# Gate inputs of a GRU stored in memory by group of columns, in two parts, and loaded back as pieces of 6144 bytes

## The chip, the cores and the metric

The kernel runs on one core of one Trainium2 chip. The metric is device microseconds of one execution; several executions are timed and the median is given. Engines are named as the profile names them: PE is the matrix engine (PEld its weight loads), DVE the vector engine, ACT the scalar engine, POOL the general one, SP the sync engine, which here only issues transfers (SPq).

## What is computed

Two layers with a residual each, on x of 8 sequences x 512 tokens x 256 channels. The first is a mixture of experts (a shared gated MLP plus two chosen of eight experts), the second a GRU over the 512 tokens:

```
x = x + moe(x, cond)                       # tokens are independent
Xz, Xr, Xh = x @ Wxz.T + bxz, x @ Wxr.T + bxr, x @ Wxh.T + bxh
for each of the 512 tokens, in order:
    Z = sigmoid(xz + H @ Whz.T + bhz)
    R = sigmoid(xr + H @ Whr.T + bhr)
    H_tilda = tanh(xh + R * H @ Whh.T + bhh)
    H = Z * H + (1 - Z) * H_tilda
    Y = H @ Whq.T + bhq
x = x + Y
```

Xz, Xr and Xh with their biases are called the gate inputs below. They are the only thing that the change touches.

## The kernel before, in words

Tokens go in 32 tiles of 128 rows: 8 sequences x 16 tokens (B = 8, TS = 16). Each of the 512 steps of the GRU is a chain PE, ACT, DVE, PE, ACT, DVE; between its parts PE does matmuls of the first layer for a later pair of tiles, by a table written by hand (`place_of` gives the row r of the table for tile n and step s). Every engine has its own program, in order, and waits on semaphores.

The gate inputs of tile t are made one tile ahead of the scan. PE projects them into two banks (`project`, L962), DVE adds the bias of each half of the columns and writes it to `xproj` (`add_bias`, L761; q is 0 or 1, PIECES = 2, each time `xp_ready` goes up by one). `xproj` has 128 partitions, one for each token, and 4 groups of 192 columns (NG = 4, RW = 192; half q is groups 2q and 2q+1). The scan needs them the other way: `xs` holds sequence b of group j on partition 32 j + b, with the 16 tokens side by side. So SP stores `xproj` to a tensor in memory and loads it back in that form, in two halves of eight tokens (`gate_rows`, L409, four transfers for a half, one for each group). `xproj`, `xs` and others lie in the tensor that the profile calls gru_raw.

ACT copies a step's row of `xs` to the banks: `seed_r` (L535) for the reset gate, `seed_zc` (L543) for the others; PE adds the products with H to it. Before the first row of a tile is copied ACT waits for `xs_first`, before row 8 for `xs_second`. The first row of tile n+1 is copied in the last step of tile n. In ACT's program the copy stands between tanh of the update gate (L595) and the step's a_row (L604), on which DVE waits.

For an odd n the halves q = 0 and q = 1 of tile n+1 come in steps 9 and 11 of tile n (`BIAS2` rows 3 and 5), for an even n in steps 0 and 1 (rows 10 and 11). Half 0 of `xs` may be overwritten once step 7 is done, half 1 once the tile is.

Of the kernel before, what the change touches and what calls it, by code (L numbers as in the profile page):

```python
# [17 lines left out]
def moe_then_gru(nc, x, cond, router_w, router_b, w1, w3, w2, we1, we2,  # L18
                 wxz, bxz, whz, bhz, wxr, bxr, whr, bhr, wxh, bxh, whh, bhh, whq, bhq, out):
    F32 = mybir.dt.float32  # L20
# [5 lines left out]
    B, T, C = x.shape  # L26
    P = 128
# [9 lines left out]
    NG = 4  # L37
# [3 lines left out]
    GATES = 3  # L41
    RW = GATES * GW
# [4 lines left out]
    HALF = TS // 2  # L47

    ctx = ExitStack()
    with ctx:  # L50
# [3 lines left out]
        def sem(name):  # L54
            return ctx.enter_context(nc.semaphore(name))
# [60 lines left out]
        xproj = spent[:, 0:NG * RW].rearrange("p (j c) -> p j c", j=NG)  # L116
# [23 lines left out]
        r_ps, z_ps, c_ps = r_bank[:, 0:GW], zc_bank[:, 0:GW], zc_bank[:, GW:2 * GW]  # L140
        tr_ps = [r_bank, zc_bank]

        by_token = nc.dram_tensor("gate_inputs_by_token", [P, NG, RW], F32, kind="Internal").ap()


        ld_x = [sem(f"ld_x{i}") for i in range(2)]
# [23 lines left out]
        bias_ready = sem("bias_ready")  # L170
# [9 lines left out]
        x1T_ready = [sem(f"x1T_ready{i}") for i in range(2)]  # L180
        xp_done = sem("xp_done")
        xp_ready = sem("xp_ready")
        xp_stored = sem("xp_stored")
        xs_first = sem("xs_first")
        xs_second = sem("xs_second")

# [54 lines left out]
        def evacuate(m):  # L241

            kind, i = GROUPS[m]
            src = tr_ps[m % 2]
            if kind == "x":
                return xT_all[:, 2 * i:2 * i + 2, :, :].rearrange("p n k t -> p (n k t)"), src[:, 0:512], 1.0
            if kind == "cond":
                return condT[:, :, :].rearrange("p k t -> p (k t)"), src[:, 0:C], 1.0
            _, part, gate = WEIGHTS[i]
            s = WSCALE[part][gate]  # L250
            if part == "x":
                return wxT[:, :, :, COLS[gate]], src[:, 0:KC * C].rearrange("p (k j n) -> p k j n", k=KC, j=NG), s
            if part == "h":
                return whT[:, gate, :, :].rearrange("p k c -> p (k c)"), src[:, 0:KC * C], s
            return wqT[:, :, :].rearrange("p k c -> p (k c)"), src[:, 0:KC * C], s
# [12 lines left out]
        PIECES = 2  # L268
# [83 lines left out]
        def iterations(body):  # L352

            for n in range(NT + 1):
                body(n, *stages(n))
# [4 lines left out]
        @block.sync  # L360
        def _(sp):
            def load_x(i, tiles):

                for n in range(tiles.start, tiles.stop):
                    sp.dma_start(x_all[:, n, :], x[:, n * TS:(n + 1) * TS, :]).then_inc(ld_x[i], 16)

            def load_gru(r):

                sp.dma_start(raw[r][:, :, :], gru_w[r].rearrange("(o p) c -> p o c", p=P)).then_inc(ld_gru, 16)

            load_x(0, slice(0, 2))
            sp.dma_start(w1_raw, w1.rearrange("(k p) h -> p k h", p=P)).then_inc(ld_w13, 16)
            sp.dma_start(w3_raw, w3.rearrange("(k p) h -> p k h", p=P)).then_inc(ld_w13, 16)
            load_x(1, slice(2, EARLY))
            sp.dma_start(rw_sb[:, :, :], router_w.rearrange("(k p) e -> p k e", p=P)).then_inc(ld_router, 16)
            sp.dma_start(cond_tok[:, :], cond.rearrange("b (a c) -> b a c", a=1).to_broadcast([B, TS, C])).then_inc(ld_router, 16)
            sp.dma_start(rbias[:, :], router_b.rearrange("(a e) -> a e", a=1).to_broadcast([P, NE])).then_inc(ld_router, 16)
            sp.dma_start(we1_raw, we1.rearrange("e (k p) h -> p e k h", p=P)).then_inc(ld_we1, 16)
            sp.wait_ge(consts_ready, 1)
            for j in range(NG):  # L380
                sp.dma_start(h0_rows[Q * j:Q * j + B, :, :], cond[:, GW * j:GW * (j + 1)].rearrange("b (i q) -> b i q", i=NI)).then_inc(ld_h0, 16)
            for r, _, _ in WEIGHTS:
                load_gru(r)
            sp.dma_start(w2_sb[:, :, :], w2.rearrange("(k p) c -> p k c", p=P)).then_inc(ld_w2, 16)
            sp.dma_start(we2_sb[:, :, :, :], we2.rearrange("e (k p) c -> p e k c", p=P)).then_inc(ld_we2, 16)
            for gate in range(GATES):
                for dst, src in ((bias_rows, gate_bx[gate]), (bias_h, gate_bh[gate])):
                    sp.dma_start(dst[:, :, COLS[gate]], src.rearrange("(a j n) -> a j n", a=1, j=NG)
                                 .to_broadcast([P, NG, GW])).then_inc(ld_bias, 16)
            sp.dma_start(bias_q[:, :], bhq.rearrange("(a c) -> a c", a=1).to_broadcast([P, C])).then_inc(ld_bias, 16)  # L390

            def load_late(t):

                for j in range(NG):
                    for b in range(2):
                        for k in range(KC):
                            src = x[b::2, t * TS:(t + 1) * TS, k * P + Q * j:k * P + Q * (j + 1)].rearrange("i t c -> t i c")
                            sp.dma_start(x_blocks[Q * j + TS * b:Q * j + TS * (b + 1), t % 2, k, :]
                                         .rearrange("t (i c) -> t i c", i=NG), src).then_inc(ld_late[t % 2], 16)
                sp.dma_start(x_all[:, t, :], x[:, t * TS:(t + 1) * TS, :]).then_inc(ld_late[t % 2], 16)  # L400

            load_late(EARLY)
            load_late(EARLY + 1)

            def gate_rows(half, done):

                for j in range(NG):
                    src = by_token[:, j, :].rearrange("(b t) c -> b t c", b=B)[:, half * HALF:(half + 1) * HALF, :]
                    sp.dma_start(xs[Q * j:Q * j + B, half * HALF:(half + 1) * HALF, :], src).then_inc(done, 16)  # L409

            sp.wait_ge(xp_ready, PIECES)
            sp.dma_start(by_token, xproj[:, :, :]).then_inc(xp_stored, 16)
            sp.wait_ge(xp_stored, 16)
            sp.wait_ge(xs_zeroed, 1)
            gate_rows(0, xs_first)
            gate_rows(1, xs_second)
            sp.wait_ge(shared_ready, NSH)
            sp.wait_ge(we1_split, NE)

            def store_out(t):  # L420

                sp.wait_ge(y_ready, t + 1)
                sp.dma_start(out[:, t * TS:(t + 1) * TS, :], y_out[:, :]).then_inc(out_stored, 16)

            def body(n, scan, proj, outs):
                if n % 2 == 0 and n > 0:
                    store_out(n - 2)
                if proj:
                    t = n + 1
                    sp.wait_ge(xp_ready, PIECES * (t + 1))  # L430
                    sp.wait_ge(xs_second, 16 * NG * t)
                    sp.dma_start(by_token, xproj[:, :, :]).then_inc(xp_stored, 16)
                    sp.wait_ge(xp_stored, 16 * (t + 1))
                if proj:
                    sp.wait_ge(seeded_zc, TS * n + HALF)
                    gate_rows(0, xs_first)
                if n % 2 == 0 and n > 0:
                    store_out(n - 1)
                if proj:
                    sp.wait_ge(seeded_zc, TS * (n + 1))  # L440
                    gate_rows(1, xs_second)
                if n % 2 == 0 and n + EARLY + 2 < NT:
                    sp.wait_ge(late_xT_ready, n + 2)
                    load_late(n + EARLY + 2)
                    load_late(n + EARLY + 3)

            iterations(body)
            sp.wait_ge(out_stored, 16 * NT)

# [177 lines left out]
        def _(dve):  # L627
# [124 lines left out]
            def add_bias(t, q):  # L752

                dve.wait_ge(xp_done, PIECES * t + q + 1)
                if q == 0:
                    if t == 0:
                        dve.wait_ge(bias_ready, GATES)
                    else:
                        dve.wait_ge(xp_stored, 16 * t)
                cols = slice(q * PCOLS, (q + 1) * PCOLS)  # L760
                dve.tensor_tensor(xproj[:, :, :].rearrange("p j c -> p (j c)")[:, cols], dn_ps[q][:, 0:PCOLS],  # L761
                                  bias_rows[:, :, :].rearrange("p j c -> p (j c)")[:, cols], ALU.add).then_inc(xp_ready, 1)
# [68 lines left out]
            for q in range(PIECES):  # L831
                add_bias(0, q)
# [20 lines left out]
            def body(n, scan, proj, outs):  # L853
                for s in range(TS):
# [39 lines left out]
                    if r in BIAS2 and 0 <= 2 * p + BIAS2[r][1] < NT:  # L894
                        add_bias(2 * p + BIAS2[r][1], BIAS2[r][0])
# [315 lines left out]
```

## Time and profile before

| | |
|---|---|
| median of 3 executions | 1314.22 us (1314.08 to 1318.01) |
| the profiled execution | 1317.0 us, of it 1315.2 us span |
| busy | PE 97%, DVE 76%, ACT 61%, PEld 67%, POOL 1% |
| granted clock of PE, mean | 0.997 |
| moved by transfers | 51.39 MB, 39 GB/s on average |
| store of the gate inputs | 32 transfers of 384 KB, 2.4 us to landing (median) |
| loads of the gate inputs | 256 transfers of 48 KB |

The span is the time from the first to the last instruction on the core; the rest of the execution's time lies around it. Busy shares are means over a start of 75 us in which the first tiles and the weights are made ready, and a scan of 512 steps. In a wait, the name behind the arrow is what ended it.

### The profile page before, as it was taken

The numbers are of one execution on the slowest core, as the hardware profiler recorded it, in microseconds if no ns is written. First come the engines' busy times: TensorE is split into PE (matmuls) and PEld (weight loads), VectorE is DVE, ScalarE is ACT, GpSimd is POOL, SyncE is SP. The second block draws the span as 40 slices with busy tenths as digits, with TensorE's granted clock in tenths as the row PEclk, the third lists the DMA queues.
The fourth block names the chain that finished last, engine by engine and source line by source line (L and its number), as shares of the span: only waits on it lengthen the run. The fifth ranks groups of instructions, "written<-read, shape, count | busy, mean of one in ns | idle before, by whom it ended". The sixth has DMA issues, their size and how long they took to land.

```text
span 1315.2 us, 85216 instructions
## 1 busy us (share of the span) xinstructions
PE 1275.3 (97%) x36022; PEld 876.9 (67%) x36022; DVE 1005.0 (76%) x6121; ACT 799.5 (61%) x4384; POOL 7.6 (1%) x26
## 2 busy tenths in 40 slices
PE   8999999999999999999999999999999999999886
PEld 7667676767767676776767667666766767676443
DVE  3567878788787878778787877878787787877765
ACT  4156666666666666666666666666666666666554
POOL 1000000000000000000000000000000000000000
PEclk8999999999999999999999999999999999999999
DMA  8111112012111101211111121111111111010110
GB/s 266 33 45 22 48 23 43 25 30 51 25 50 23 42 25 30 50 25 49 23 39 30 30 51 24 50 21 37 33 30 44 25 43 30 18 38 14 44 20 11
DMA packets 79252, 51.39 MB, mean 39 GB/s; under 512 B 43032, under 2 KB 74264, under 8 KB 78872
## 3 DMA queue, kind: packets, MB, share of 16 engines
q1 hardware_dynamic: 78872, 45.95, 14.7%
q8 instruction: 284, 4.65, 1.6%
q14 instruction: 96, 0.79, 0.2%
HBM read 29.13 MB, written 16.78 MB: 35 GB/s over the span
## 4 chain that ended last, share of the span: by engine, by line
PE 88%; DVE 5%; ACT 3%; DMA 2%; issue 1%; SPq 0%
PE dn_ps L962 27%; PE up_ps L989 24%; PE zc_bank L1099 20%; PE r_bank L1099 14%; PE aux L962 2%; DVE terms L882 2%; DMA gru_raw<-gate_inputs_by_token 1%; ACT t_r L593 1%; DVE hist L885 1%; ACT t_h L613 1%; DVE t_rT L862 1%; PE misc L962 1%; DMA gate_inputs_by_token<-gru_raw 1%; DMA xT_all<-in_L_cond_w 1%; DVE factors L868 0%
## 5 line engine op out<-in xcount | busy, mean ns | idle before, releaser
L593 ACT ACTIVATE t_r<-r_bank 128x32 f32<-128x32 f32 x1024 | 146.2, 195 | 227.5 <-PE r_bank L1099 213.7
L962 PE MATMUL dn_ps<-we_sb,hid_e 128*32 128x256 f32 (+1 forms) x5176 | 281.3, 335 | 1.7 <-DVE x_all L748 1.2
L862 DVE STREAM_TRANSPOSE t_rT<-t_r 128x32 f32<-128x32 f32 x1024 | 156.0, 190 | 158.2 <-ACT t_r L593 148.8
L613 ACT ACTIVATE t_h<-zc_bank 128x32 f32<-128x32 f32 x1024 | 146.1, 195 | 210.2 <-PE zc_bank L1099 210.2
L1099 PEld LDWEIGHTS zc_bank<-whT,rhT 128*8 128x8 f32 x8192 | 119.1, 87 | 183.9 <-DVE rhT L865 179.9
L1099 PE MATMUL r_bank<-whT,hist 128*8 128x64 f32 x8192 | 212.2, 220 | 20.8 <-DVE hist L885 15.4
L1099 PE MATMUL zc_bank<-whT,rhT 128*8 128x64 f32 x8192 | 212.9, 220 | 4.7 <-issue 0.6
L1099 PE MATMUL zc_bank<-whT,hist 128*8 128x64 f32 x8192 | 209.8, 219 | 0.2 <-issue 0.2
L1099 PEld LDWEIGHTS r_bank<-whT,hist 128*8 128x8 f32 x8192 | 118.8, 88 | 125.9 <-DVE hist L885 99.9
L882 DVE STREAM_TRANSPOSE terms<-t_h 128x32 f32<-128x32 f32 x1024 | 156.8, 192 | 55.1 <-ACT t_h L613 20.0
L962 PEld LDWEIGHTS dn_ps<-we_sb,hid_e 128*32 128x32 f32 x5176 | 141.4, 110 | 37.8 <-DVE x_all L748 3.1
L543 ACT ACTIVATE zc_bank<-gru_raw 128x128 f32<-128x128 f32 x512 | 144.3, 282 | 16.0
L989 PE MATMUL up_ps<-x_high,we_low 128*128 128x256 f32 x512 | 152.7, 298 | 0.0
L989 PE MATMUL up_ps<-x_low,we_high 128*128 128x256 f32 x512 | 152.6, 298 | 0.0
L989 PE MATMUL up_ps<-x_high,we_high 128*128 128x256 f32 x512 | 151.8, 296 | 0.4 <-issue 0.4
L885 DVE TENSOR_TENSOR_SCAN hist<-factors,terms 128x16 f32<-128x16 f32 x1024 | 145.5, 184 | 0.0
L1099 PEld LDWEIGHTS zc_bank<-whT,hist 128*8 128x8 f32 x8192 | 143.3, 90 | 0.5 <-issue 0.4
L868 DVE STREAM_TRANSPOSE factors<-a_row 128x64 f32<-128x64 f32 x512 | 126.2, 246 | 21.5 <-ACT a_row L604 2.5
L865 DVE SCALAR_TENSOR_TENSOR rhT<-t_rT,hist 128x8 f32<-128x8 f32 x1024 | 133.4, 168 | 0.0
L748 DVE SCALAR_TENSOR_TENSOR x_all<-dn_ps,gates_all,x_all 128x256 f32<-128x256 f32 x256 | 119.5, 471 | 15.4 <-PE dn_ps L962 11.6
L604 ACT ACTIVATE a_row<-t_z 128x64 f32<-128x64 f32 x512 | 125.7, 246 | 0.1
L535 ACT ACTIVATE r_bank<-gru_raw 128x64 f32<-128x64 f32 x512 | 114.3, 223 | 4.0 <-DMA gru_raw<-gate_inputs_by_token 4.0
(114 smaller groups left out, 1664.0 us busy)
## 6 DMA issues: line engine op xcount, KB each, us to landing
gate_inputs_by_token<-gru_raw SPq DMA_DIRECT2D x32, 384.0 KB, 2.4
gru_raw<-gate_inputs_by_token SPq DMA_DIRECT2D x256, 48.0 KB
xT_all<-in_x SPq DMA_DIRECT2D x448, 8.0 KB
x_all<-in_x SPq DMA_DIRECT2D x32, 128.0 KB
out<-gru_raw SPq DMA_DIRECT2D x32, 128.0 KB
x_all<-in_L_cond_W1e SPq DMA_DIRECT2D x1, 2048.0 KB, 12.1
we_sb<-in_L_cond_W2e SPq DMA_DIRECT2D x1, 2048.0 KB, 13.0
xT_all<-in_L_cond_w SPq DMA_DIRECT2D x2, 512.0 KB, 6.2
```

Of the source, the lines that this page charges most:

```text
L543: act.activation(zc_bank[:, 0:2 * GW], xs[:, s, GW:RW], ACT.Copy).then_inc(seeded_zc, 1)
L593: act.activation(t_r[:, i, :], r_ps[:, i * Q:(i + 1) * Q], ACT.Tanh, scale=0.5).then_inc(tr_ready, 1)
L604: act.activation(a_row[:, :, :], t_z[:, :, :], ACT.Copy, bias=0.5, scale=-0.5).then_inc(a_ready, 1)
L613: act.activation(t_h[:, i, :], c_ps[:, i * Q:(i + 1) * Q], ACT.Tanh, scale=-1.0).then_inc(th_ready, 1)
L862: dve.transpose(t_rT[:, i, :], t_r[:, i, :]).then_inc(trT_done, 1)
L865: dve.scalar_tensor_tensor(rhT[:, i, :], t_rT[:, i, 0:B], 1.0, old[:, i, :], ALU.add, ALU.mult)\
L868: dve.transpose(factors[:, :, :, 1].rearrange("p i q -> p (i q)"), a_row[:, :, :].rearrange("p i q -> p (i q)"))\
L882: dve.transpose(terms[:, i, :, 0], t_h[:, i, :]).then_inc(thT_done, 1)
L885: dve.tensor_tensor_scan(hist[:, s, i, :, :].rearrange("p b e -> p (b e)"), factors[:, i, 0:B, :].rearrange("p b e -> p (b e)"), terms[:, ...
L962: done = pe.matmul(ps[Q * j:Q * (j + 1), col:col + cols], lhsT[:, Q * j:Q * (j + 1)], rhs, start=first, stop=last, tile_position=(0, Q * j ...
L989: done = pe.matmul(up_ps[place % 2][:, half * PAIR:(half + 1) * PAIR], w, (x_low if low_x else x_high)[:, p % 2, :, k, :], start=(m % UP_M ...
L1099: done = pe.matmul(ps[Q * j:Q * j + B, :], lhsT[:, k, :], whT[:, gate, k, j * GW:(j + 1) * GW], start=False, stop=(k == NI - 1), tile_posi ...
```

## The change

The tensor in memory is laid out by group first, then token, then column. The store goes in two transfers, one for each half q, each issued when DVE has written that half. It then writes 768 bytes in one run for each token and group (before: 3072 bytes for each token). A load of one group and half of the tokens reads, for each sequence, eight tokens that now lie side by side: 8 runs of 6144 bytes (before: 64 of 768 bytes). Its loads wait for the store of their own half of the groups. The wait for the loads of the tile before now stands ahead of the wait for `xp_ready`, and DVE waits for each half's own earlier store before it overwrites it.

```diff
-        by_token = nc.dram_tensor("gate_inputs_by_token", [P, NG, RW], F32, kind="Internal").ap()
+        by_group = nc.dram_tensor("gate_inputs_by_group", [NG, P, RW], F32, kind="Internal").ap()
-        xp_stored = sem("xp_stored")
+        xp_stored = [sem(f"xp_stored{q}") for q in range(2)]
-            def gate_rows(half, done):
-
-                for j in range(NG):
-                    src = by_token[:, j, :].rearrange("(b t) c -> b t c", b=B)[:, half * HALF:(half + 1) * HALF, :]
+            def store_inputs(t, q):
+
+                groups = slice(q * NG // PIECES, (q + 1) * NG // PIECES)
+                sp.wait_ge(xp_ready, PIECES * t + q + 1)
+                sp.dma_start(by_group[groups, :, :].rearrange("j p c -> p j c"), xproj[:, groups, :]).then_inc(xp_stored[q], 16)
+
+            def gate_rows(q, half, done):
+
+                for j in range(q * NG // PIECES, (q + 1) * NG // PIECES):
+                    src = by_group[j, :, :].rearrange("(b t) c -> b t c", b=B)[:, half * HALF:(half + 1) * HALF, :]
                     sp.dma_start(xs[Q * j:Q * j + B, half * HALF:(half + 1) * HALF, :], src).then_inc(done, 16)
...
-            sp.wait_ge(xp_ready, PIECES)
-            sp.dma_start(by_token, xproj[:, :, :]).then_inc(xp_stored, 16)
-            sp.wait_ge(xp_stored, 16)
+            for q in range(PIECES):
+                store_inputs(0, q)
             sp.wait_ge(xs_zeroed, 1)
-            gate_rows(0, xs_first)
-            gate_rows(1, xs_second)
+            for q in range(PIECES):
+                sp.wait_ge(xp_stored[q], 16)
+                gate_rows(q, 0, xs_first)
+            for q in range(PIECES):
+                gate_rows(q, 1, xs_second)
...
                 if proj:
-                    t = n + 1
-                    sp.wait_ge(xp_ready, PIECES * (t + 1))
-                    sp.wait_ge(xs_second, 16 * NG * t)
-                    sp.dma_start(by_token, xproj[:, :, :]).then_inc(xp_stored, 16)
-                    sp.wait_ge(xp_stored, 16 * (t + 1))
-                if proj:
+                    sp.wait_ge(xs_second, 16 * NG * (n + 1))
+                    for q in range(PIECES):
+                        store_inputs(n + 1, q)
                     sp.wait_ge(seeded_zc, TS * n + HALF)
-                    gate_rows(0, xs_first)
+                    for q in range(PIECES):
+                        sp.wait_ge(xp_stored[q], 16 * (n + 2))
+                        gate_rows(q, 0, xs_first)
...
-                if q == 0:
-                    if t == 0:
-                        dve.wait_ge(bias_ready, GATES)
-                    else:
-                        dve.wait_ge(xp_stored, 16 * t)
+                if t > 0:
+                    dve.wait_ge(xp_stored[q], 16 * t)
+                elif q == 0:
+                    dve.wait_ge(bias_ready, GATES)
```

What SP issues for one tile of the scan, before (an odd n; L432 is the store, L409 the loads; in brackets the semaphores waited for ahead of a transfer):

```order
L432 DMA gate_inputs_by_token<-gru_raw 128x768 [waits xs_second,xp_ready]
L409 DMA gru_raw<-gate_inputs_by_token 8x8x192 [waits seeded_zc,xp_stored]
L409 DMA gru_raw<-gate_inputs_by_token 8x8x192 x3
L409 DMA gru_raw<-gate_inputs_by_token 8x8x192 [waits seeded_zc]
L409 DMA gru_raw<-gate_inputs_by_token 8x8x192 x3
```

And what it issues there now (L409 is now the store, L415 the loads; 8x1536 is eight runs of 1536 numbers):

```order
L409 DMA gate_inputs_by_group<-gru_raw 128x2x192 [waits xp_ready,xs_second]
L409 DMA gate_inputs_by_group<-gru_raw 128x2x192 [waits xp_ready]
L415 DMA gru_raw<-gate_inputs_by_group 8x1536 [waits xp_stored0,seeded_zc]
L415 DMA gru_raw<-gate_inputs_by_group 8x1536
L415 DMA gru_raw<-gate_inputs_by_group 8x1536 [waits xp_stored1]
L415 DMA gru_raw<-gate_inputs_by_group 8x1536
L415 DMA gru_raw<-gate_inputs_by_group 8x1536 [waits seeded_zc]
L415 DMA gru_raw<-gate_inputs_by_group 8x1536 x3
```

The first store waits only for the first half of `xproj`, both stores stand ahead of the first load, and the last two loads of the first half wait for the second store. The number of loads is the same. On DVE nothing moves; the second half of the bias now has a wait of its own. DVE's instructions around it for the second half of tile 1 (L761 before, L768 now), before:

```order
L885 SCALAR_TENSOR_TENSOR hist<-factors,terms 128x16 [waits thT_done] x2
L761 TENSOR_TENSOR gru_raw<-dn_ps,bias_rows 128x384 [waits xp_done]
L862 STREAM_TRANSPOSE t_rT<-t_r 128x32 [waits tr_ready] x2
```

And now:

```order
L892 SCALAR_TENSOR_TENSOR hist<-factors,terms 128x16 [waits thT_done] x2
L768 TENSOR_TENSOR gru_raw<-dn_ps,bias_rows 128x384 [waits xp_stored1,xp_done]
L869 STREAM_TRANSPOSE t_rT<-t_r 128x32 [waits tr_ready] x2
```

Behind the bias stands the first transpose of the next step of the scan in both.

## Rows read from the trace of the kernel before

**Rows 1.** The page: busy time of each engine (share, instructions).

```profile
PE 1275.3 (97%) x36022; PEld 876.9 (67%) x36022; DVE 1005.0 (76%) x6121; ACT 799.5 (61%) x4384; POOL 7.6 (1%) x26
```

**Rows 2.** Waits, whole span: us in total, times, longest.

```profile
ACT r_bank L535 <- DMA gru_raw<-gate_inputs_by_token: 4.0, 2, 2.7
PE r_bank L1099 <- ACT r_bank L535: 1.1, 1, 1.1
```

**Rows 3.** Timeline, 58 to 84: start, us, instruction, count, [idle before].

```profile
64.83 0.56 DVE L761 TENSOR_TENSOR gru_raw<-dn_ps,bias_rows 128x384 f32<-128x384 f32 x1 [1.74 <-PE dn_ps L962]
...
66.12 0.56 DVE L761 TENSOR_TENSOR gru_raw<-dn_ps,bias_rows 128x384 f32<-128x384 f32 x1 [0.73 <-PE dn_ps L962]
...
72.10 1.50 PE L962 MATMUL dn_ps<-wxT,x1T 128*32 128x384 f32 x16
...
74.39 0.23 ACT L535 ACTIVATE r_bank<-gru_raw 128x64 f32<-128x64 f32 x1 [2.75 <-DMA gru_raw<-gate_inputs_by_token]
...
74.67 0.41 PE L1099 MATMUL r_bank<-whT,hist 128*8 128x64 f32 x16 [1.08 <-ACT r_bank L535]
```

**Rows 4.** Chain that ended last, 55 to 90: start, us, what.

```profile
66.70 2.33 DMA gate_inputs_by_token<-gru_raw
69.05 0.27 SPq L409
...
70.07 4.30 DMA gru_raw<-gate_inputs_by_token
```

**Rows 5.** Chain that ended last, 675 to 693, end of tile 15.

```profile
681.32 2.41 DMA gate_inputs_by_token<-gru_raw
...
684.75 4.15 DMA gru_raw<-gate_inputs_by_token
...
688.93 0.23 ACT r_bank L535
```

**Rows 6.** Timeline of ACT, 148 to 152.9, last two steps of tile 1.

```profile
148.01 0.22 ACT L595 ACTIVATE t_z<-zc_bank 128x64 f32<-128x64 f32 x1
148.13 0.22 ACT L535 ACTIVATE r_bank<-gru_raw 128x64 f32<-128x64 f32 x1
...
150.43 0.22 ACT L595 ACTIVATE t_z<-zc_bank 128x64 f32<-128x64 f32 x1
150.65 0.23 ACT L535 ACTIVATE r_bank<-gru_raw 128x64 f32<-128x64 f32 x1
```

**Rows 7.** Chain that ended last, 985 to 1005, end of tile 23.

```profile
992.24 3.42 DMA gate_inputs_by_token<-gru_raw
...
996.69 4.37 DMA gru_raw<-gate_inputs_by_token
```

**Rows 8.** Timeline of all engines there, 998 to 1003.5.

```profile
1001.08 0.23 ACT L535 ACTIVATE r_bank<-gru_raw 128x64 f32<-128x64 f32 x1 [1.27 <-DMA gru_raw<-gate_inputs_by_token]
...
1002.55 0.41 PE L1099 MATMUL r_bank<-whT,hist 128*8 128x64 f32 x16 [1.29 <-DVE hist L885]
```

**Rows 9.** SP's transfers, 60 to 1315: start, us to issue all, count.

```profile
66.70 0.36 SPq L412 DMA_DIRECT2D gate_inputs_by_token<-gru_raw  x1
...
527.35 0.35 SPq L432 DMA_DIRECT2D gate_inputs_by_token<-gru_raw  x1
530.32 5.18 SPq L409 DMA_DIRECT2D gru_raw<-gate_inputs_by_token  x8
...
1226.68 5.49 SPq L409 DMA_DIRECT2D gru_raw<-gate_inputs_by_token  x8
1232.21 0.62 SPq L423 DMA_DIRECT2D out<-gru_raw  x1
```

**Rows 10.** Busy time in stretches at the start; last: clock, DMA share, GB/s.

```profile
66.70:69.00 2.30, 1.88 (x23) 0.97 (x21) 0.96 (x3) 0.38 (x1) 0.00 (x0) 1.00 0.42 171
69.05:70.30 1.25, 0.98 (x9) 0.98 (x9) 0.97 (x3) 0.00 (x0) 0.00 (x0) 1.00 0.10 22
70.30:74.40 4.10, 3.30 (x32) 2.08 (x30) 1.20 (x3) 0.77 (x3) 0.00 (x0) 1.00 0.57 74
```

**Rows 11.** The stores: time to landing, least, median and most.

```profile
DMA to landing us min/median/max: 2.3/2.4/3.9
```

**Rows 12.** Waits of PE, 90 to 1300, that no releaser explains.

```profile
PE r_bank L1099 <- issue: 1.4, 1, 1.4
PE zc_bank L1099 <- issue: 0.8, 3, 0.5
PE dn_ps L962 <- issue: 0.4, 1, 0.4
PE up_ps L989 <- issue: 0.4, 2, 0.2
```

More of the change, by code:

```diff
@@ L440, in body @@
                     sp.wait_ge(seeded_zc, TS * (n + 1))
-                    gate_rows(1, xs_second)
+                    for q in range(PIECES):
+                        gate_rows(q, 1, xs_second)
                 if n % 2 == 0 and n + EARLY + 2 < NT:
```

## The prediction

> **What bounds the kernel now.** I read the page first: PE is busy for 1275.3 us, 97% of the span, in [rows 1]. A change that moves only transfers can therefore give back only time in which PE stands still because of them. So the list of waits comes next. In the whole span the first copy of a tile's gate inputs (L535) found ACT idle for the loads twice, 4.0 us in all, 2.7 us the longest, and PE waited once for such a copy directly, 1.1 us [rows 2]. The other one has to reach PE by a longer way, so I looked for both in the timeline and in the chain of work that ended last.
>
> The first is at the start. The two biases of tile 0 end at 65.39 and 66.68. The store goes out at 66.70 and lands 2.33 us later; the four loads of the first half go out from 69.05, the fourth at 70.07, and that one lands 4.30 us after its issue, at 74.37 [rows 3, 4]. ACT copies at 74.39, PE begins the scan at 74.67, after 1.08 us of idleness: its last earlier work, the projection from 72.10, is through after 1.50 us, at 73.60 [rows 3].
>
> The second is at the end of tile 23. There the store took 3.42 us to land and the fourth load 4.37 us [rows 7], ACT was idle 1.27 us, and the update of H came late, so that PE stood still for 1.29 us before the next step [rows 8]. All tiles with odd n have this chain, since their second bias comes only in step 11. It runs in 2.41 + 3 x 0.34 + 4.15 = 7.58 us at the end of tile 15 (the 0.34 is a third of 69.05 to 70.07) [rows 4, 5], and in 8.82 us at tile 23 (992.24 to 1001.06) [rows 7]. At a usual end the copy starts 0.22 us after the tanh ahead of it, in a step without the wait 0.12 us [rows 6]: the loads land some 0.1 us late even then, and PE does not wait, since ACT's copy is small and something else ends that part of the step. So the ordinary case has no slack and no loss, and each microsecond above about 7.6 us costs about one: 1.24 us more gave 1.29 us. There are 15 such ends (n = 1, 3, ... 29). For even n the loads go out in the middle of the tile and are in place long before they are wanted.
>
> **The change part by part.** Work on PE, ACT and DVE is the same, instruction for instruction. What changes is when the last load of a first half lands.
>
> *At the start.* The first store can go at 65.41 instead of 66.70. The trace has no store of half the size with 768-byte runs. From below I take the shortest store, 2.3 us [rows 11]; from above 3.42 us [rows 7], since half the bytes in twice as many runs for each byte should not exceed the slowest that I followed. I use 2.33 us, nearest in place and in what runs beside it. The second store is issued at 66.70 as before, and lands at 69.03. Its issue may take SP longer than the 0.36 us of a store now: a transfer whose memory side has three dimensions took 0.62 us [rows 9]. It is over by 67.4, before the first store lands at 67.74, so nothing waits for it. The first two loads go at about 67.76 and 68.10, ahead of the second store's landing. The last two follow at 69.05 and 69.39: 0.68 us earlier than the fourth load goes now, because two issues of 0.34 us have been moved into a wait.
>
> How long the last two then take is the unknown that matters. In the 1.25 us after the first load's issue the transfer engines are almost idle (share 0.10), in the 4.10 us until landing they are at 0.57 [rows 10]: a lead time, then data. If half of the data is through before, the rest takes 1.25 + 4.1 / 2 = 3.3 us. That is my value. The upper bound is that nothing improves, 4.30 us [rows 4]; the lower the shortest store, 2.3 us [rows 11]. Landing is then at 69.39 + 3.3 = 72.7 us, with the upper bound at 73.7 us. PE can use the copy from 73.60 on, if the landing is 0.30 us ahead (74.37 to 74.67), at 73.30 [rows 3, 4]. So 72.7 us removes the whole 1.08 us, and even 73.7 us removes 0.7 us. More than 1.08 us isn't there to be had.
>
> Eight runs of 6144 bytes in place of 64 of 768 should help the transfer engines if they are held up by the number of runs. They are above half busy while moving only 74 GB/s, where the store phase moved 171 GB/s at a lower share, 0.42 [rows 10]. The difference is either the small runs or the place they go to: a load reaches only eight partitions, before and after. Since the gap closes with 3.3 us already, I cost this part at nothing; what would hide its gain is PE's own work up to 73.60.
>
> The Trainium skill, page SBUF — State Buffer, section "Door 1: The DMA port swizzle", says that partitions four at a time, and the same ones 32 further on, share one of 16 ports, so that groups 0 and 1 would go into the same two ports, and groups 2 and 3 into two others; the page DMA: Bandwidth & Descriptors, section "Where 436 GB/s comes from", puts a port at 27.2 GB/s. By that rule longer runs bring little: an estimate from the two pages is 98 KB / 54.4 GB/s = 1.8 us for each pair of groups, whatever the run. The low rate at a high share speaks for the rule, and nothing in this trace separates it from the runs.
>
> *In the scan.* From the second bias on, the new chain is 2.41 + 0.34 + 3.3 = 6.05 us, against 7.58 us. With a store as slow as that at tile 23, 3.42 us, it is 7.06 us, still under 7.6 us. So the 1.29 us goes too. The ordinary ends gain nothing, since PE doesn't wait there. The new first wait on SP (for the earlier loads) holds up nothing: these were issued at the last tile's end. DVE's new wait for the second half's store comes in step 11 or step 1, a whole tile after that store landed. If this cover were gone, the transpose behind it would stand still, and the scan with it.
>
> *Sum.* Against the profiled execution: 1317.0 - 1.08 - 1.29 = 1314.6 us (1315.2 span becomes 1312.8). It ran 2.8 us above the median of the three others, 1314.22 us, and I can't see whether these had the late end at tile 23. I count half of it: 1314.22 - 1.08 - 0.65 = 1312.5 us. A difference below 0.3%, 3.9 us, can't be told from none in a measurement of this kernel.
>
> **The rivals.**
>
> *The loads take as long as now (4.30 and 4.15 us).* The runs make no difference, and half the bytes ahead makes none either, because the two pairs go different ways or wait for one another. For it: the few partitions. Against: the first pair is issued 1.3 us earlier. The start gives 0.7 us. In the scan 2.41 + 0.34 + 4.15 = 6.90 us, and with a slow store 7.91 us, 0.33 us over; counted half as above, (1.29 - 0.33) / 2 = 0.5. Time: 1313.0 us.
>
> *Nothing is gained.* The store of the second half is late by as much as is saved, or some other work of PE's at the start becomes the next to be late. Time: 1314.2 us.
>
> *Slower: the second store is late in every odd tile.* Its packets go with the first two loads, which are issued right behind it, and its short runs could make it as slow as 3.42 us every time, its issue 0.27 us longer (0.62 for 0.35) [rows 9]. With loads of 4.37 us the chain is 3.42 + 0.27 + 0.34 + 4.37 = 8.40 us, 0.82 us above 7.58 us, at 15 ends: +12.3 us, 1326.5 us. It decides from a chain of 7.58 us on, and is seen in the measurement from 7.84 us (3.9 / 15 = 0.26). For it: there is no slack. Against: it needs both ends at once, and the trace has a store and its loads slow together at one end only [rows 7].
>
> *Faster by over 0.3%.* PE's instructions arrive late a few times between 90 and 1300 us, together 3.0 us by what no releaser explains [rows 12]. If that comes from the traffic of small packets, it may go as well: 1314.22 - 1.08 - 1.29 - 3.0 = 1308.9 us. Against: the rows tie these waits to no transfer, and the bytes are the same.
>
> **How the numbers follow.** Forecast 0.60 (own range 1311.5 to 1313.5); loads no faster 0.17; nothing gained 0.12; slower 0.05; faster 0.06. The first three all lie within 0.3%, so faster 0.06, same 0.89, slower 0.05. The range is 1309.5 to 1316.5 us: below, most of the way to the faster case; above, nothing gained together with most of the 2.8 us by which single executions of the same kernel differ.
>
> **What would show it.** Right: two stores, the first issued at about 65.4 us and both landing in 2.3 to 2.6 us; no idle time of ACT before L535 (a new line number) for the loads; PE's gap of 1.08 us before the first step under 0.1 us, the first step at about 73.6 us; no gap at an end of an odd tile; PE's busy time unchanged within 1 us. Steps of the scan stay as long as they are. Wrong: a store above 3.4 us to landing, loads above 4.4 us, ACT idle ahead of the first copy at many odd tiles, or DVE idle ahead of its bias for a store. The forecast's size fails if PE is held at the start by something other than the copy, or if the four executions timed differ in the unexplained waits by more than the 1.7 us at stake.

## The result, and the profile after

The changed kernel runs in 1309.87 us (median of 6, 1307.01 to 1310.87). The kernel before has a median of 1315.9 us over 6 executions (1314.08 to 1318.8), the first three among them. The ratio is 0.9945, 95% interval 0.9929 to 0.9960: faster by 5 to 9 us, some 6 to 7 us, where 1.7 us was forecast. Ratios leave out four executions far from all others: two of `store_whole` at 1360 us, one of `split_only` at 5827 us, one of the kernel before at 1810 us.

The page after, its span, busy times, first queue and the transfers of the gate inputs (KB each, us to landing):

```profile
span 1305.2 us, 85279 instructions
...
PE 1269.7 (97%) x36022; PEld 873.1 (67%) x36022; DVE 1005.3 (77%) x6121; ACT 799.2 (61%) x4384; POOL 7.3 (1%) x26
...
q1 hardware_dynamic: 77336, 45.95, 13.8%
...
gate_inputs_by_group<-gru_raw SPq DMA_DIRECT2D x64, 192.0 KB, 2.0
```

Timeline of the start after:

```profile
63.75 0.56 DVE L768 TENSOR_TENSOR gru_raw<-dn_ps,bias_rows 128x384 f32<-128x384 f32 x1 [1.74 <-PE dn_ps L969]
64.34 1.67 SPq L409 DMA_DIRECT2D gate_inputs_by_group<-gru_raw  x2
65.04 0.56 DVE L768 TENSOR_TENSOR gru_raw<-dn_ps,bias_rows 128x384 f32<-128x384 f32 x1 [0.73 <-PE dn_ps L969]
66.41 3.15 SPq L415 DMA_DIRECT2D gru_raw<-gate_inputs_by_group  x8
71.02 1.50 PE L969 MATMUL dn_ps<-wxT,x1T 128*32 128x384 f32 x16
71.33 0.23 ACT L543 ACTIVATE r_bank<-gru_raw 128x64 f32<-128x64 f32 x1 [0.76 <-DMA gru_raw<-gate_inputs_by_group]
...
72.33 0.41 PE L1106 MATMUL r_bank<-whT,hist 128*8 128x64 f32 x16
```

The second bias starts at 65.04, where it was 66.12 [rows 3]: that 1.08 us lies ahead of the changed code, in a part that differs from execution to execution. From there ACT's copy comes 6.29 us later, where it was 8.27 us; PE has no gap, and begins the scan 7.29 us after it, where it was 8.55 us. ACT still waits 0.76 us for the loads, but PE has work of its own until 72.5.

The whole scan can be measured from the first tanh of an update gate (L595 before, L603 after) to the last of the 512, in ACT's timeline. Before, then after:

```profile
75.37 0.22 ACT L595 ACTIVATE t_z<-zc_bank 128x64 f32<-128x64 f32 x1
...
1307.67 0.22 ACT L595 ACTIVATE t_z<-zc_bank 128x64 f32<-128x64 f32 x1
```

```profile
73.03 0.22 ACT L603 ACTIVATE t_z<-zc_bank 128x64 f32<-128x64 f32 x1
...
1297.68 0.22 ACT L603 ACTIVATE t_z<-zc_bank 128x64 f32<-128x64 f32 x1
```

That is 1232.3 and 1224.65 us: 7.65 us inside the scan in this pair of executions, though one late end of 1.3 us is all that the list of waits for the loads showed there. Waits of PE from 90 us on, after, with no releaser:

```profile
PE up_ps L996 <- issue: 0.2, 1, 0.2
```

Before they were 3.0 us [rows 12]. What this looks like is seen in the kernel before at 867.5 us, in the chain of work that ended last, in step 8 of tile 20. PE stops in the middle of 16 matmuls that wait for no semaphore:

```profile
867.30 0.23 PE r_bank L1099 x8
867.53 1.41 issue
868.94 0.30 PE r_bank L1099 x8
```

Four loads of gate inputs had gone out at 862.36. The transfer engines' share (last but one) in the stretches ahead of the stop:

```profile
863.00:864.00 1.00, 1.00 (x39) 0.52 (x28) 0.82 (x7) 0.69 (x5) 0.00 (x0) 1.00 0.34 89
864.00:865.00 1.00, 1.00 (x31) 0.87 (x32) 0.86 (x7) 0.57 (x3) 0.00 (x0) 1.00 0.57 71
865.00:866.00 1.00, 1.00 (x51) 0.67 (x42) 0.74 (x5) 0.71 (x5) 0.00 (x0) 1.00 0.40 53
866.00:867.00 1.00, 1.00 (x25) 0.89 (x22) 0.79 (x7) 0.53 (x5) 0.00 (x0) 1.00 0.00 0
```

The trace also shows what PE waits for there: its own instructions, which come by transfers too. The queue `instruction` of the page before, and what the queues did just ahead of the stop, from 865 to 867.5 us (packets, MB, share of 16 engines):

```profile
q8 instruction: 284, 4.65, 1.6%
```

```profile
q1 hardware_dynamic: 55, 0.04, 11.1%
q8 instruction: 1, 0.02, 5.0%
```

Each of the 284 packets has 16,384 bytes. PE runs 72,849 instructions (36,022 matmuls, as many weight loads, 805 others), 256.5 for each packet. The one packet here starts at 865.45 and takes 1.98 us (5.0% of 16 x 2.5 us), the longest of the 284, whose median is 1.13 us; PE goes on 1.51 us after its end. The same holds for every such wait: between 90 and 1300 us the twenty traces of this document have 65 of them, 26.4 us in all. Each stands at the same place of a block of 256 PE instructions and ends 1.2 to 1.7 us after a packet of this queue.

Packets beside other transfers are slow more often. Of 2654 packets in the scan that ran with no other transfer, 6 took more than 1.5 us and none more than 1.8 us; of 2830 that ran beside others, 101 and 28 did. The kernel before has 8 and 6 packets above 1.5 us in its two traces, `no_transfers`, which leaves out the transfers of the gate inputs in the scan, has 1. The six waits above 0.8 us all follow packets of 1.83 to 1.98 us. But 35 of the 65 waits follow packets below 1.5 us, so slow packets are not all of it.

The waits are not the whole delay either, for a matmul's modelled end hides part of it as busy time. Taking the five intervals between matmul starts about each end of a block, and the median of the twenty traces for each interval, the kernel before is 7.5 us late there and the changed one 1.6 us. So 5.9 of the 7.65 us lie at the ends of blocks: 2.8 us as idle time, and 3.1 us as busy time, by which PE's busy time within the scan is shorter in the changed kernel.

### The profile page after: what moved, and what is told of

Same layout as the page of the kernel before. It is cut to its first block, busy times and chain, and to the rows that moved or that the text cites. A ratio compares the mean times of both kernels' runs of the same rounds, so it can differ in the third digit from the quotient of the medians.

```text
span 1305.2 us, 85279 instructions
## 1 busy us (share of the span) xinstructions
PE 1269.7 (97%) x36022; PEld 873.1 (67%) x36022; DVE 1005.3 (77%) x6121; ACT 799.2 (61%) x4384; POOL 7.3 (1%) x26
## 3 DMA queue, kind: packets, MB, share of 16 engines
q1 hardware_dynamic: 77336, 45.95, 13.8%
## 4 chain that ended last, share of the span: by engine, by line
PE 89%; DVE 5%; ACT 3%; SPq 1%; issue 1%; DMA 1%
PE dn_ps L969 28%; PE up_ps L996 25%; PE zc_bank L1106 20%; PE r_bank L1106 14%; PE aux L969 2%; DVE terms L889 2%; ACT t_r L601 1%; ACT t_h L621 1%; DVE hist L892 1%; DVE t_rT L869 1%; PE misc L969 1%; DMA w_sb<-in_L_cond_w 1%; SPq L381 1%; DVE gru_raw L719 0%; DVE factors L875 0%
## 5 line engine op out<-in xcount | busy, mean ns | idle before, releaser
L1106 PE MATMUL r_bank<-whT,hist 128*8 128x64 f32 x8192 | 210.9, 220 | 16.9 <-DVE hist L892 13.8
```

The costliest lines, as they stand in the source:

```text
L1106: done = pe.matmul(ps[Q * j:Q * j + B, :], lhsT[:, k, :], whT[:, gate, k, j * GW:(j + 1) * GW], start=False, stop=(k == NI - 1), tile_posi ...
```

## The experiments

Two theories were set against each other. *Waits*: the gain is the gap at the start and late ends of odd tiles. *Traffic*: the transfers, above all their short runs, keep PE from its instructions, and the change eases that. The kernels come in five sets; those of a set were timed on one chip beside the kernel before, and share its times. Sets 2 and 3 were on the same chip, the others each on another. A ratio of 0.001 is 1.3 us. In the table the ratio, its interval, and from each kernel's one trace: the scan's length as above, ACT's wait for loads from 90 us on, and PE's waits without releaser there (the sum of the lines of the view, which are rounded to 0.1), all in us.

| kernel | ratio | interval | scan | ACT | PE |
|---|---|---|---|---|---|
| before (first trace) | 1 | | 1232.3 | 1.3 | 3.0 |
| changed (first trace) | 0.9945 | 0.9929-0.9960 | 1224.65 | 0 | 0.2 |
| *set 1* after_again | 0.9940 | 0.9927-0.9953 | 1224.66 | 0 | 0.2 |
| before_again | 0.9999 | 0.9985-1.0012 | 1228.45 | 1.0 | 2.3 |
| split_only | 0.9941 | 0.9925-0.9957 | 1225.9 | 0 | 1.4 |
| layout_only | 0.9988 | 0.9976-1.0000 | 1230.7 | 1.0 | 2.3 |
| *set 2* no_transfers | 0.9955 | 0.9940-0.9969 | 1225.5 | 0 | 0.6 |
| traffic_768 | 0.9991 | 0.9976-1.0005 | 1225.65 | 0 | 0.7 |
| traffic_6144 | 0.9951 | 0.9934-0.9968 | 1224.4 | 0 | 0.5 |
| split_together | 0.9976 | 0.9964-0.9988 | 1226.1 | 0.2 | 1.6 |
| *set 3* store_whole | 0.9958 | 0.9943-0.9972 | 1224.9 | 0 | 0.5 |
| store_halves | 0.9931 | 0.9915-0.9948 | 1223.3 | 0 | 0.4 |
| loads_768 | 0.9970 | 0.9957-0.9982 | 1223.1 | 0 | 0 |
| late_loads | 1.0130 | 1.0111-1.0148 | 1252.6 | 24.2 | 1.3 |
| *set 4* split_start | 0.9995 | 0.9980-1.0009 | 1232.0 | 3.1 | 2.9 |
| split_scan | 0.9981 | 0.9969-0.9992 | 1224.6 | 0 | 0.2 |
| split_at_end | 0.9996 | 0.9986-1.0006 | 1228.35 | 0 | 1.6 |
| split_at_begin | 0.9999 | 0.9988-1.0011 | 1230.05 | 2.6 | 2.4 |
| *set 5* split_all_b | 0.9956 | 0.9939-0.9973 | 1225.6 | 0 | 1.3 |
| split_scan_b | 0.9966 | 0.9954-0.9978 | 1227.7 | 0 | 3.0 |

### Set 1: the two halves of the change

`split_only` keeps memory by token and splits the store (runs of 1536 bytes); `layout_only` lays memory out by group but stores once.

```diff
 # split_only, against the changed kernel (by_token is [P, NG, RW] again)
-                sp.dma_start(by_group[groups, :, :].rearrange("j p c -> p j c"), xproj[:, groups, :]).then_inc(xp_stored[q], 16)
+                sp.dma_start(by_token[:, groups, :], xproj[:, groups, :]).then_inc(xp_stored[q], 16)
 # layout_only, against the kernel before (at both stores)
-            sp.dma_start(by_token, xproj[:, :, :]).then_inc(xp_stored, 16)
+            sp.dma_start(by_group.rearrange("j p c -> p j c"), xproj[:, :, :]).then_inc(xp_stored, 16)
```

after_again: 

> The changed kernel once more, as a control for the three runs beside it. Waits theory (the gain is PE's gap at the start and late ends of odd tiles): 5 to 7 us under the kernel before, 1309 to 1311. Traffic theory (short runs delay PE's instructions): the same time; in its trace the scan's 511 steps take under 1226 us, where the kernel before had 1232 us.

before_again: 

> The kernel before once more, for a second trace and for how far two runs of one kernel differ. Both theories: ratio 1.000 within 0.002. Waits theory: at several ends of odd tiles the copy of the first row finds ACT idle for the loads, together 3 to 6 us. Traffic theory: at most one such end; PE idle with no releaser for 2 us or more in all, as before (3.0 us).

split_only: 

> Two stores, but memory laid out by token as before (loads in runs of 768 bytes). Waits theory: all that the waits cost is gone, since the chain from the second bias is about 0.7 us shorter or more: 5 to 7 us faster than before. Traffic theory: only the 1.1 us at the start and a late end, 1 to 2.5 us faster.

layout_only: 

> One store as before, but memory laid out by group (loads in runs of 6144 bytes, store in runs of 768). Waits theory: loads faster by 1 us or so, the chain under 7.6 us, most of the gain: 4 to 6 us faster. Traffic theory: 4 to 6 us faster too, with PE's unexplained waits gone and its gap of 1.1 us at the start partly kept. Told apart from the waits theory by the pair with the split alone.

The split alone gives the whole gain, the runs of 6144 bytes alone give 0 to 3 us. Why so little is seen in the chain of `layout_only` at the end of tile 23, and in its list of transfers:

```profile
991.72 3.42 DMA gate_inputs_by_group<-gru_raw
...
996.16 3.90 DMA gru_raw<-gate_inputs_by_group
```

```profile
gate_inputs_by_group<-gru_raw SPq DMA_DIRECT2D x32, 384.0 KB, 2.8
```

A load lands in 3.90 us where it took 4.37 us [rows 7], but the store, now in runs of 768 bytes, takes 2.8 us in the median where it took 2.4 us. Over all 15 ends of odd tiles the median of the fourth load goes from 3.87 to 3.56 us, and the median time from the second bias to the last landing from 7.40 to 7.37 us. What one side of the memory gains the other gives back. With the split that time is 5.48 us (`split_only`) and 5.49 us (the changed kernel). Both theories had expected 4 to 6 us of `layout_only` and missed; of `split_only` the waits theory had expected 5 to 7 us, the traffic theory 1 to 2.5 us, and 7.8 us came. `before_again` shows one late end, not the several that the waits theory had expected, and 2.3 us of PE's unexplained waits; neither fits the waits theory as put.

### Set 2: the same traffic without its waits

`no_transfers` leaves out the store and the loads in the scan; `traffic_768` keeps them as in the kernel before, `traffic_6144` as in the changed one, but their loads go to a part of `xT_all` that is no longer used. In all three every tile uses tile 0's gate inputs. `split_together` is the changed kernel with both stores issued once both halves are ready.

```diff
 # all three: ACT waits for the loads of tile 0 alone (edits of other waits that go with it are left out here)
-                        if s + 1 == HALF:
-                            act.wait_ge(xs_second, 16 * NG * (n + 1))
-                        if last:
-                            act.wait_ge(xs_first, 16 * NG * (n + 2))
+                        if s + 1 == HALF and n == 0:
+                            act.wait_ge(xs_second, 16 * NG)
 # the two with traffic: the loads in the scan go to spare
+        spare = late_xT[:, 0:TS * RW].rearrange("p (t c) -> p t c", t=TS)
-                    sp.dma_start(xs[Q * j:Q * j + B, half * HALF:(half + 1) * HALF, :], src).then_inc(done, 16)
+                    sp.dma_start(to[Q * j:Q * j + B, half * HALF:(half + 1) * HALF, :], src).then_inc(done, 16)
 # split_together
-                sp.wait_ge(xp_ready, PIECES * t + q + 1)
+                sp.wait_ge(xp_ready, PIECES * (t + 1))
```

no_transfers: 

> The kernel before, with the gate inputs of tile 0 used for every tile: no store and no load of gate inputs in the scan, none waited for; the start as before. It shows what all these transfers cost. Waits theory and traffic theory alike: the gap of 1.1 us at the start stays, all else that the transfers cost goes, so about 5.5 us faster than before (0.996).

traffic_768: 

> The kernel before, its stores and loads issued as before, but in the scan the loads go to a part of xT_all that is no longer used and ACT waits for none of them (it uses the gate inputs of tile 0 for every tile). Waits theory: as fast as the kernel without these transfers, 4.5 to 5.5 us under before. Traffic theory: the traffic is the same, so only the late end of tile 23 goes: 1 to 1.5 us under before (0.999).

traffic_6144: 

> The changed kernel with its loads in the scan going to the same unused place and not waited for. Waits theory: the same as the changed kernel within 1 us (no wait is left there to lose). Traffic theory: the same too; under the loads in runs of 768 bytes without waits by 4 to 5 us.

split_together: 

> The changed kernel, but both stores wait for both halves and go out together. If only being earlier counts, the start keeps about half of its gain and each end of an odd tile is 7.0 to 7.6 us after the second bias: 3 to 5 us faster than before. If two small stores in place of a large one count by themselves, nearly all the gain stays: 5.5 to 6.5 us faster.

Without any of these transfers 4 to 8 us go (0.9955), with the same traffic unawaited only -1 to 3 us (0.9991). So by these times the waits in the scan of the kernel before are worth some 1.2 us, as the traffic theory said, and the rest goes with the traffic. But `traffic_6144`, which has the split start too, is as fast as the changed kernel: that one's transfers cost next to nothing. One thing doesn't fit: the trace of `traffic_768` has a scan as short as that of the kernel without transfers, and its time lies at the start (its second bias begins 2.3 us later than in [rows 3]), so one trace and twelve times do not tell the same. `split_together` is 1.6 to 4.7 us faster than before, as expected if only being earlier counts: two small stores in place of a large one do not give the gain by themselves. The traffic theory's own step, that the short runs do it, had already fallen with `split_only`, whose loads have runs of 768 bytes.

### Set 3: the store alone, the loads alone, and the price of a late end

```diff
 # in all but late_loads every tile uses tile 0's gate inputs, as above; waits that go with it are left out here
 # store_whole: the loads in the scan are left out of the kernel before
-                    gate_rows(0, xs_first)
-                    gate_rows(1, xs_second)
 # store_halves: the same in split_only; loads_768: the store in the scan is left out of traffic_768
-                    sp.dma_start(by_token, xproj[:, :, :]).then_inc(xp_stored, 16)
 # late_loads, against the changed kernel
-                    sp.wait_ge(seeded_zc, TS * n + HALF)
+                    sp.wait_ge(seeded_zc, TS * n + (TS - 1 if n % 2 == 1 else HALF))
```

store_whole: 

> The kernel before with one store of 384 KB for each tile of the scan, but no loads there and none waited for (the gate inputs of tile 0 are used for every tile). Large-store theory (a store of 384 KB in one piece holds back what PE needs, waits count for little): slower than the kernel without transfers by 3 to 5 us, 1 to 3 us under before. Loads theory (the loads of 768-byte runs do it): as fast as without transfers, 5 to 6 us under before.

store_halves: 

> The same with two stores of 192 KB, each when its half is ready (runs of 1536 bytes), no loads in the scan. Its start has the split too, worth 1.3 us. Large-store theory: 3 to 5 us faster than with the whole stores apart from the start, so 6 to 7 us under before. Loads theory: only the start differs, 1.3 us under the kernel with whole stores.

loads_768: 

> The kernel before with its loads of 768-byte runs for each tile of the scan, to the unused place and not waited for, but no stores there. Large-store theory: as fast as without transfers, 5 to 6 us under before. Loads theory: 1 to 2 us under before.

late_loads: 

> The changed kernel with the loads of the first half held back in the odd tiles until the scan is at step 14, so that they land some 2 us after they are wanted. It prices a late end. If each microsecond of lateness costs one: PE idle before the first step of 15 tiles, 1.5 to 2.5 us each, 22 to 38 us slower than the changed kernel, 1.2% to 2.4% slower than before. If the scan can take up lateness, less than 10 us.

The large-store theory falls: the whole store alone costs nothing that can be told (0.9958 beside 0.9955 without any). `store_halves` is 3.5 us faster still, of which the start explains 1.3 us; the intervals leave the rest between nothing and some 5 us. With the loads alone 3.9 of the 5.9 us are still gained. By the medians of the ratios neither part alone costs what both together do in `traffic_768`, but the intervals of `loads_768` and `traffic_768` overlap.

`late_loads` gives a clean price. Its waits from 90 us on:

```profile
PE r_bank L1106 <- DVE hist L892: 36.3, 45, 2.9
...
ACT r_bank L543 <- DMA gru_raw<-gate_inputs_by_group: 24.2, 15, 2.9
```

15 ends, all late, 24.2 us of ACT's idleness; PE's waits for the update of H grow from 13.8 us (the changed kernel) by 22.5 us, and the kernel is slower than `after_again` by 23.8 us (1332.86 less 1309.02, two sets). A microsecond of lateness costs one, and not more: PE's waits without releaser stay at 1.3 us with 15 late ends.

### Sets 4 and 5: the split in one place alone

```diff
 # against split_only; split(t) is t == 0, t > 0, t even and > 0, t odd; split_all_b is split_only again
             def store_inputs(t, q):
+                if not split(t):
+                    if q == 0:
+                        sp.wait_ge(xp_ready, PIECES * (t + 1))
+                        sp.dma_start(by_token, xproj[:, :, :]).then_inc(xp_stored[0], 16)
+                    return
...
```

split_start: 

> Only the first tile's store is split; the scan is as before. Waits theory: 1.3 us faster than before (0.999), the bias of tile 0 at the same time. If the start holds more than the wait: 2.5 us or more.

split_scan: 

> All stores but the first tile's are split. Waits theory (the late end of tile 23 alone): 1 to 1.5 us faster. If the scan holds the rest: 5 to 6 us faster (0.996), its 511 steps in 1224 to 1226 us.

split_at_end: 

> Only the stores of tiles 2, 4, ... are split, whose inputs are ready in steps 9 and 11 just before they are wanted. If late ends and what follows from them are the cause: all of the scan's gain, 5 us. If the traffic itself holds PE back wherever it falls: half of it, 2 to 3 us.

split_at_begin: 

> Only the stores of tiles 1, 3, ... are split, whose inputs are ready in steps 0 and 1 of the tile before and wanted 14 steps later. Waits theory: no gain, within 0.7 us of before. If the traffic itself holds PE back: 2 to 3 us.

split_all_b: 

> The split everywhere, memory by token. If the parts add up and the earlier difference came from the calls: 4 to 5 us faster than before, 1.3 us faster than its neighbour. If the parts together give more than their sum: 6 to 7.5 us faster than before, 3 us or more faster than its neighbour.

split_scan_b: 

> The split in the scan alone. In either case 2.5 to 3.5 us faster than before, as in the last call; 5 to 6 us only if that call was off.

The split in the scan is worth 2.5 us in one set and 4.5 us in the other, the start 0.7 us by its own kernel and 1.3 us as the difference of the last two; together 3 to 6 us, and the split everywhere 5.8 us in this last set, 7.8 us in the first. Within the intervals the parts add up; no single place holds the gain. The two halves of the scan apart, 0.5 and 0.1 us, are both below what can be told, and fall short of the 2.5 us that they have together by less than their intervals. That `split_at_end` gives only -0.8 to 1.8 us was expected by neither theory (5 us, or 2 to 3 us).

The traces add what the times can't. The two kernels whose scan (or its ends) is not split have more late ends than any trace before, `late_loads` apart. ACT's waits from 90 us on, of `split_start`, then of `split_at_begin`:

```profile
ACT r_bank L558 <- DMA gru_raw<-gate_inputs_by_token: 3.1, 3, 1.8
```

```profile
ACT r_bank L558 <- DMA gru_raw<-gate_inputs_by_token: 2.6, 4, 1.1
```

And in the fourteen traces with the split at the ends, or with no loads awaited there (`late_loads` apart), there is none but 0.2 us in `split_together`.

The late ends keep to their places. In all five traces with a whole store awaited at the ends, tile 23 is one of them: PE stood still there for 1.29, 0.98, 0.80, 0.97 and 0.96 us, and the store took 3.15 to 3.42 us, where the median is 2.4 us (2.8 us in `layout_only`). In the changed kernel it still takes 3.05 us there, but ends early enough. The two other long ones, 1.87 and 1.11 us, are both at tile 19. Why the store is slow at these places no run shows.

## Why the prediction was wrong

**Right.** *The start*: PE's gap of 1.08 us is gone, and the copy comes 1.98 us sooner after the second bias. The traces with the split start have no gap, but for 0.4 us in `split_together`, whose two stores go out together; those without it have 0.9 to 1.3 us. The new last wait was not the copy but PE's own work, as forecast. *The mechanism of a late end*: next to no slack, and a price of one for one, shown by `late_loads`. (Not quite none: the loads "some 0.1 us late even then" were read at tile 1, one of six ends where ACT waited; at the nine others they landed 0.1 to 0.4 us ahead of the copy.) *The shorter chain*: 5.49 us in the median, forecast 6.05 us. *The runs of 6144 bytes at nothing*: `layout_only` 0 to 3 us, `split_only` as fast as the whole change. *No end is late after the change.* One sign did not hold: PE's busy time was to stay within 1 us and fell from 1275.3 to 1269.7 us, 3.1 us of it in the scan, where late instructions had lengthened it.

**Wrong in size: the late ends.** The step was "I count half of it", 0.65 us, from one late end in one trace. The five traces in which whole stores are awaited at the ends have 1.3, 1.0, 1.0, 3.1 and 2.6 us of such waits, 1.8 us on average; one execution can have three or four. Some 1.0 us of it is tile 23, late in every one of the five, so that halving it had no ground; the rest is ends that the first trace did not show. By the times the late ends are worth less, 1.2 us (`traffic_768`) and 0.5 us (`split_at_end`), both with intervals that reach to nothing. A chain with next to no slack is late wherever one of its parts is slow, and one trace is a poor count of that.

**Wrong in kind: "Against: the rows tie these waits to no transfer".** That put the case of more than 0.3% at 0.06. In those same five traces PE waits 3.0, 2.3, 2.3, 2.9 and 2.4 us with no releaser, 2.6 us on average, and the scan takes 1230.7 us; in the fourteen others with these ends split, unawaited or left out, apart from `late_loads`, the waits average 0.9 us and the scan 1225.3 us. So the change took most of the 3.0 us of [rows 12] too, which only the rival had priced. This term stood at nothing in the forecast. The rows of the views tie these waits to no transfer, but the trace does: each ends just after a packet of PE's own instructions. Counted as in the section on the result, with what hides in busy time, the five traces are 5.8 us late at the ends of blocks on average, the fourteen 2.5 us.

**The sum, as measured.** The start 1.1 to 1.3 us (traces); late ends 1.8 us on average (traces; 1.2 us by the time of `traffic_768`); late instructions 3.3 us (traces: 5.8 less 2.5), of which 1.7 us stand in the list of waits (2.6 less 0.9). That makes 6.3 us, where 6 to 7 us were measured. The scan's averages differ by 5.4 us, and the last two terms explain 5.1 us of it. The forecast had 1.08, 0.65 and nothing.

**The base was off too.** The three executions before had a median of 1314.22 us, six have 1315.9 us. Part of the distance from 1.7 to 7 us is that; the time itself, 1309.87 us, lies just within the range, and the ratio does not.

**Open.** What PE waits for is shown; what about a whole store, awaited at the ends, makes it wait more often is not. By the delay at the ends of blocks it is not lateness alone (3.7 us in `late_loads`), not the whole store alone (1.7 us in `store_whole`), not the loads alone (0.2 us in `loads_768`). The stop at 867.5 us follows a burst of loads, but the stop of 0.48 us that ends at 858.98 us follows a packet of 0.96 us, with no other transfer near. The five traces range from 4.4 to 7.5 us, and two with split ends, `split_at_end` and `split_scan_b`, have 5.1 and 5.2 us. With one trace for each kernel the tie to the split is a correlation of 19 traces, found after the fact; the kernel whose traffic is whole and unawaited argues for the traffic by its times and against it by its trace.

## What to carry to other kernels

Where a chain is in place just as it is wanted, count it as late some of the time: take the spread of its parts' landing times over all its occurrences, not the waits of one trace, and ask whether a late one comes at the same place in a second trace. Here, splitting a store so that its first part goes while the second is computed shortened such a chain by 1.9 us and the new layout alone by nothing, for it lengthened the runs of the loads and shortened those of the store. And waits "without releaser" are part of what a change in the traffic can move: look among the packets of the queue `instruction` for what ended them, and give them more than a few chances in a hundred when the change touches every tile.

## What the runs showed of the hardware

A store of 384 KB lands in 2.4 us in runs of 3072 bytes and in 2.8 us in runs of 768 bytes; a store of 192 KB in 1.9 us in runs of 1536 bytes (`split_only`) and in 2.0 us in runs of 768 bytes, so half the bytes save 0.5 to 0.8 us only. The fourth load of 48 KB at the ends of odd tiles takes 3.87 us in the median with runs of 768 bytes and 3.56 us with runs of 6144 bytes (`layout_only`); at the end of tile 23 it took 4.37 and 3.90 us. Eight times fewer and longer runs gain 0.3 to 0.5 us.

The Trainium skill, page SBUF — State Buffer, section "Door 1: The DMA port swizzle", says that a transfer's bandwidth depends on how many of 16 ports its partitions reach; by its table the eight partitions of a load reach two. If that is the limit, longer runs should bring little, and the small gain agrees with it; no run here changed the number of partitions.

PE's instructions come in packets of 16,384 bytes, 256 instructions each, which take 1.13 us in the median (kernel before) and up to 1.98 us beside other transfers. When one is late PE stands still, 65 times in twenty traces, and goes on 1.2 to 1.7 us after the packet's end.
